# Another order for the head of a four-stage kernel: weights ahead of x, another order of the loads, ten warm-up calls

## The reference, cut to what matters

```
attn = (w1^T @ w2^T) * sparse_mask                       # 512 x 512
x = x + gelu(layernorm(x) @ attn + b2)                   # stage 1
x = x + ffn(layernorm(x))                                # stage 2
x = x + attention(layernorm(x); Wqkv, bqkv, Wo, bo)      # stage 3, one head of 128
x = x + ffn(layernorm(x))                                # stage 4

ffn(z): dots = softmax(z @ centroids.T / 0.1); hits = dots > 0.01
        rows where any hit, columns whose cluster was hit anywhere:
        z @ weight.T + bias, else 0
```

## Time and profile before

| | before |
|---|---|
| median of 3 runs | 275.45 us |
| the profiled execution, its own time | 275.24 us |
| its span | 273.4 us |
| TensorE busy | 268.8 us (98%) |
| DVE, ACT, POOL busy | 192.2, 177.0, 163.8 us |
| HBM read, written | 13.76 MB, 4.19 MB |

### The profile page before, as it was taken

The page is one execution under the profiler, slowest core; times in us unless marked ns, Lnnn a source line. Parts: engine busy times, 40 slices in busy tenths (PEclk is TensorE's granted clock), DMA queues, the critical chain, the costliest instruction groups (busy, mean ns, idle before and its releaser), DMA issues.

```text
span 273.4 us, 4428 instructions
## 1 busy us (share of the span) xinstructions
PE 268.8 (98%) x1397; PEld 225.6 (82%) x1397; DVE 192.2 (70%) x406; ACT 177.0 (65%) x359; POOL 163.8 (60%) x196
## 2 busy tenths in 40 slices
...
DMA packets 10247, 18.25 MB, mean 67 GB/s; under 512 B 1200, under 2 KB 1968, under 8 KB 10224
## 3 DMA queue, kind: packets, MB, share of 16 engines
...
HBM read 13.76 MB, written 4.19 MB: 66 GB/s over the span
## 4 chain that ended last, share of the span: by engine, by line
PE 96%; DMA 1%; DVE 1%; POOL 1%; issue 0%; ACT 0%; DVEq 0%; POOLq 0%
PE m_bank L1018 76%; PE t_bank L1113 12%; PE m_bank L1197 6%; PE t_bank L1119 1%; DMA x_tok<-in_L_attn_a_x 1%; PE m_bank L1073 1%; ACT xn_odd L613 0%; PE t_bank L1138 0%; DVE st L817 0%; POOL rstd L471 0%; POOL ve L470 0%; DVE y_tok L988 0%; DVE x_tok L994 0%; PE m_bank L1144 0%; PE t_bank L1124 0%
## 5 line engine op out<-in xcount | busy, mean ns | idle before, releaser
L1018 PE MATMUL m_bank<-ffn_hi,even_hi 128*128 128x512 f32 x96 | 38.9, 406 | 0.0
L1018 PE MATMUL m_bank<-ffn_lo,even_hi 128*128 128x512 f32 x96 | 37.6, 392 | 0.0
L1018 PE MATMUL m_bank<-ffn_hi,even_lo 128*128 128x512 f32 x96 | 37.4, 390 | 0.0
L602 ACT ACTIVATE ones_and_squares<-x_tok,mv 128x512 bf16<-128x512 f32 x44 | 31.6, 717 | 4.1 <-DVE x_tok L921 3.7
L559 POOL TENSOR_TENSOR y_tok<-y_tok,x_tok 128x512 f32<-128x512 f32 x12 | 15.3, 1289 | 25.6 <-ACT y_tok L755 25.6
L539 POOL TENSOR_TENSOR y_tok<-y_tok,bias_f 128x512 f32<-128x512 f32 x16 | 20.6, 1295 | 16.2 <-ACT y_tok L696 16.2
L467 POOL TENSOR_SCALAR ve<-mv 128x1 f32<-128x1 f32 (+1 forms) x20 | 5.3, 264 | 37.9 <-ACT ones_and_squares L602 36.9
L824 DVE TENSOR_TENSOR even_lo<-t_bank,even_hi 128x512 fp32r<-128x512 f32 x24 | 16.2, 684 | 12.8 <-ACT even_hi L645 12.6
L471 POOL TENSOR_TENSOR rstd<-ve,half 128x1 f32<-128x1 f32 (+1 forms) x31 | 23.5, 758 | 2.6
L824 DVE TENSOR_TENSOR odd_lo<-t_bank,odd_hi 128x512 fp32r<-128x512 f32 x28 | 18.8, 686 | 6.4 <-ACT odd_hi L645 6.2
L1018 PE MATMUL m_bank<-odd_hi,wqkv_hi 128*128 128x512 f32 (+1 forms) x60 | 21.5, 358 | 0.0
...
## 6 DMA issues: line engine op xcount, KB each, us to landing
...
```

The costliest lines, as they stand in the source:

```text
L602: act.activation(squares, x_tok[:, n, :], ACT.Square, bias=sum_of(*key), scale=-float(D), accum_out=mv[:, i, 1:2]).then_inc(done[kind], 1)
L1018: ins = pe.matmul(bank, a, w, start=(first and n == 0), stop=(last and n == count - 1))
```

## The change

`WARM` goes from 12 to 10 and five orders are rewritten in their first part. Every step keeps its code; the set of steps is the same. From `dn2.0.1.c21` on TensorE's, from `sq.2.1.2` on ACT's, from `onehot` on DVE's and from `rstd.2.0 ... xlo.2.0` on POOL's order are unchanged. The code of ACT's first load is rewritten without changing what it issues, but it is `load.w1.1` now. `BY_POOL` is the same set.

```diff
-WARM = 12
+WARM = 10
 PE_ORDER
-attn.0.0 T.x1.0.0 attn.0.1 attn.0.2 T.x1.0.1 attn.1 T.x1.0.2 last.0 last.1 last.2 last.3 T.x1.0.3 y1.0.0.c0
-y1.0.2.c0 y1.0.0.c2 T.cen.0.0 y1.0.2.c2 y1.0.3.c02 y1.0.0.c1 colmean y1.0.0.c3 y1.0.1.c3 ffnmean y1.0.2.c1
-y1.0.1.c2 y1.0.2.c3 y1.0.1.c10 y1.0.3.c31 y1.1.0.c02 T.x2.0.2 y1.1.0.c3 y1.1.2.c0213 y1.1.0.c1 T.x2.0.0
-y1.1.1.c231 y1.1.3.c132 y1.1.1.c0 T.x2.0.3 T.x2.0.1 dn2.0.2.c01 y1.1.3.c0 dn2.0.0.c10 T.x2.1.0 dn2.0.0.c2
-dn2.0.2.c23 dn2.0.3.c32 dn2.0.0.c3 dn2.0.3.c0 dn2.0.1.c21 dn2.0.3.c1 cl2.0.h01 T.x2.1.3 y1.2.0.c20 T.x2.1.1
+attn.0.0 attn.0.1 attn.0.2 attn.1 last.0 last.1 T.x1.0.2 last.2 last.3 T.x1.0.0 T.x1.0.1 T.x1.0.3 y1.0.2.c02
+y1.0.0.c201 y1.0.3.c0 colmean y1.0.0.c3 y1.0.1.c12 y1.0.2.c31 y1.0.3.c3 y1.0.1.c30 y1.0.3.c2 T.x2.0.0 T.x2.0.2
+y1.0.3.c1 y1.1.0.c01 ffnmean y1.1.1.c012 y1.1.0.c2 y1.1.3.c01 y1.1.0.c3 y1.1.3.c23 T.x2.0.1 y1.1.1.c3
+y1.1.2.c032 T.x2.0.3 y1.1.2.c1 dn2.0.0.c203 T.cen.0.0 dn2.0.2.c01 dn2.0.0.c1 T.x2.1.0 dn2.0.2.c23 dn2.0.3.c320
+dn2.0.1.c21 dn2.0.3.c1 cl2.0.h01 T.x2.1.3 y1.2.0.c20 T.x2.1.1 dn2.0.1.c30 T.x2.1.2 y1.2.0.c3 y1.2.3.c3 y1.2.0.c1
 ACT_ORDER
-w1hi.0 w2hi.0 norm.1.0.0 w1hi.1 norm.1.0.1 w2hi.1 w2hi.2 w1hi.2 w1hi.3 w2hi.3 norm.1.0.2 hi.x1.0.0 hi.x1.0.2
-hi.x1.0.1 rawhi.0 norm.1.0.3 rawhi.2 hi.x1.0.3 ccen rawhi.1 fshi rawhi.3 shi xhi.1.0 ahi.0 gelu.0.0 ahi.2 ahi.3
-gelu.0.2 ahi.1 hi.cen.0.0 xhi.1.2 sq.2.0.2 gelu.0.3 xhi.1.3 xhi.1.1 hi.x2.0.2 gelu.0.1 fhi.2 fhi.1 sq.2.0.0
-hi.x2.0.0 fhi.0 sq.2.0.3 gelu.1.0 sq.2.0.1 gelu.1.2 fhi.3 hi.x2.0.3 gelu.1.1 hi.x2.0.1 sq.2.1.2 gelu.1.3 xhi.2.0
+w1hi.0 w1hi.1 w2hi.0 w1hi.2 w2hi.3 w2hi.1 w2hi.2 w1hi.3 norm.1.0.3 norm.1.0.2 rawhi.0 hi.x1.0.2 norm.1.0.1
+norm.1.0.0 rawhi.2 rawhi.1 hi.x1.0.0 hi.x1.0.1 hi.x1.0.3 rawhi.3 shi ahi.0 ahi.1 gelu.0.0 xhi.1.0 gelu.0.2 fshi
+ahi.2 xhi.1.1 xhi.1.2 gelu.0.3 xhi.1.3 gelu.0.1 hi.x2.0.2 hi.x2.0.0 ahi.3 fhi.0 fhi.1 fhi.2 ccen sq.2.0.1
+gelu.1.0 fhi.3 gelu.1.1 hi.x2.0.1 sq.2.0.0 hi.x2.0.3 sq.2.0.3 gelu.1.3 hi.cen.0.0 sq.2.0.2 gelu.1.2 sq.2.1.2
 DVE_ORDER
-stats.1.0.0 w1lo.0 stats.1.0.1 stats.1.0.2 w2lo.0 stats.1.0.3 w1lo.1 w2lo.1 w2lo.2 w1lo.2 w1lo.3 w2lo.3
-lo.x1.0.0 cstat lo.x1.0.1 mask_attn.0 mask_attn.1 lo.x1.0.2 mask_attn.2 rawlo.0 rawlo.2 mask_attn.3 lo.x1.0.3
...
+w1lo.0 w1lo.1 w2lo.0 w1lo.2 w2lo.3 w2lo.1 stats.1.0.3 w2lo.2 w1lo.3 stats.1.0.2 stats.1.0.1 stats.1.0.0
+mask_attn.0 mask_attn.1 rawlo.0 lo.x1.0.2 mask_attn.2 cstat mask_attn.3 rawlo.2 lo.x1.0.0 lo.x1.0.3 rawlo.1
+rawlo.3 slo lo.x1.0.1 stats.1.1.3 center.0 center.1 scaled.0.0 center.2 stats.1.1.2 scaled.0.2 x1.0.0 x1.0.2
+scaled.0.1 fslo scaled.0.3 center.3 stats.1.1.1 stats.1.2.1 x1.0.3 stats.1.1.0 x1.0.1 fcent.1 fcent.0 fcent.2
+scaled.1.0 lo.x2.0.2 fcent.3 scaled.1.1 lo.x2.0.0 scaled.1.3 x1.1.0 x1.1.1 lo.x2.0.1 scaled.1.2 stats.1.2.3
+lo.cen.0.0 stats.1.3.3 x1.1.2 lo.x2.0.3 stats.1.2.0 x1.1.3 onehot stats.1.2.2 lo.x2.1.1 scaled.2.0 lo.x2.1.0
 POOL_ORDER
-rstd.1.0.0 rstd.1.0.1 rstd.1.0.2 rstd.1.0.3 fsum.1 fsum.2 fsum.3 asum.1 cmean asum.2 asum.3 alo.0 xlo.1.0 alo.2
-alo.3 xlo.1.2 alo.1 xlo.1.3 xlo.1.1 rstd.1.1 flo.0 latehi.2 flo.1 flo.2 rstd.2.0 flo.3 xlo.2.0 latehi.0 xlo.2.2
+rstd.1.0.3 rstd.1.0.2 rstd.1.0.1 rstd.1.0.0 asum.1 asum.2 asum.3 fsum.1 fsum.2 fsum.3 alo.0 alo.1 xlo.1.0
+xlo.1.1 alo.2 cmean xlo.1.3 alo.3 rstd.1.1 xlo.1.2 flo.1 flo.2 flo.0 flo.3 latehi.4 latehi.2 rstd.2.0 xlo.2.0
 SP_ORDER
-load.x0.0 load.w2.0 load.x0.1 load.x0.2 load.w1.1 load.x0.3 load.w2.1 load.w2.2 load.w1.2 load.w1.3 load.w2.3
-load.ffn.1 load.ffn.0 load.cen load.ffn.2 load.sparse.0 load.ffn.3 load.sparse.1 load.sparse.2 load.sparse.3
-load.small load.x.1 load.b2 load.xt.1 load.x.3 load.late load.x.2 load.bias load.xt.2 load.xt.3 store.0.1
+load.w1.0 load.w2.0 load.w1.2 load.w2.3 load.w2.1 load.w2.2 load.x0.3 load.w1.3 load.x0.2 load.x0.1 load.x0.0
+load.sparse.0 load.sparse.1 load.sparse.2 load.sparse.3 load.ffn.2 load.ffn.1 load.cen load.ffn.0 load.ffn.3
+load.x.1 load.b2 load.xt.1 load.x.3 load.bias load.x.2 load.small load.late load.xt.2 load.xt.3 store.0.1
-AQ_ORDER = "load.w1.0"
+AQ_ORDER: load.w1.1
```

More of the change, by code:

```diff
@@ L25 @@
 M_BANKS = 4
-WARM = 12
-BY_POOL = {(1, 3), (2, 3), (3, 2), (2, 2)}
+WARM = 10
+BY_POOL = {(1, 3), (2, 2), (2, 3), (3, 2)}
 SQUARED = {2, 3, 4}
 PE_ORDER = """
-attn.0.0 T.x1.0.0 attn.0.1 attn.0.2 T.x1.0.1 attn.1 T.x1.0.2 last.0 last.1 last.2 last.3 T.x1.0.3 y1.0.0.c0
-y1.0.2.c0 y1.0.0.c2 T.cen.0.0 y1.0.2.c2 y1.0.3.c02 y1.0.0.c1 colmean y1.0.0.c3 y1.0.1.c3 ffnmean y1.0.2.c1
-y1.0.1.c2 y1.0.2.c3 y1.0.1.c10 y1.0.3.c31 y1.1.0.c02 T.x2.0.2 y1.1.0.c3 y1.1.2.c0213 y1.1.0.c1 T.x2.0.0
-y1.1.1.c231 y1.1.3.c132 y1.1.1.c0 T.x2.0.3 T.x2.0.1 dn2.0.2.c01 y1.1.3.c0 dn2.0.0.c10 T.x2.1.0 dn2.0.0.c2
@@ new lines @@
+dn2.0.1.c21 dn2.0.3.c1 cl2.0.h01 T.x2.1.3 y1.2.0.c20 T.x2.1.1 dn2.0.1.c30 T.x2.1.2 y1.2.0.c3 y1.2.3.c3 y1.2.0.c1
+y1.2.3.c2 y1.2.2.c13 dn2.1.0.c1 y1.2.3.c10 y1.2.1.c3 y1.2.2.c0 y1.2.1.c1 y1.2.2.c2 dn2.1.0.c0 tc.2.0 dn2.1.2.c0
+y1.2.1.c02 dn2.1.0.c23 dn2.1.2.c312 cl2.1.h01 y1.3.3.c1 dn2.1.1.c02 y1.3.3.c3 dn2.1.3.c30 tc.2.1 y1.3.2.c1
+y1.3.3.c20 y1.3.2.c3 dn2.1.1.c3 y1.3.2.c2 dn2.1.3.c1 T.x2.2.0 dn2.1.1.c1 dn2.1.3.c2 T.x2.2.2 y1.3.2.c0 y1.3.1.c2
+T.x2.2.3 y1.3.1.c13 T.x2.2.1 y1.3.0.c1 y1.3.1.c0 y1.3.0.c302 T.x2.3.3 cl2.2.h01 T.x2.3.2 T.x2.3.1 dn2.2.3.c0
@@ new lines @@
+dn2.3.3.c3 dn2.2.3.c3 T.x2.3.0 tc.2.2 dn2.3.3.c1 dn2.2.3.c21 dn2.2.0.c2 cl2.3.h0 cl2.3.h1 dn2.2.2.c3 tc.2.3
+dn2.2.2.c1 dn2.2.0.c1 dn2.2.2.c2 dn2.2.0.c03 dn2.3.3.c20 dn2.2.2.c0 bestT.2 dn2.3.1.c2 mask.2 dn2.2.1.c1
+dn2.3.2.c3 dn2.3.1.c03 dn2.2.1.c2 dn2.3.2.c20 dn2.3.1.c1 dn2.3.2.c1 dn2.2.1.c0 T.x3.0.3 dn2.3.0.c13 T.x3.0.0
+dn2.3.0.c0 T.x3.0.2 dn2.3.0.c2 T.x3.0.1 dn2.2.1.c3 k.0.h1 k.0.h0 q.0.h0 q.0.h1 v.0.h1 T.x3.1.3 v.0.h0 sc.0.0
+T.x3.1.2 T.x3.1.1 sc.0.2 T.x3.1.0 T.v.0.0 sc.0.1 sc.0.3 T.p.0.0 q.1.h01 T.p.0.1 k.1.h01 T.p.0.2 T.p.0.3 v.1.h01
@@ new lines @@
+sc.1.3 T.x3.2.3 T.x3.2.0 sc.1.2 pv.0.h01 sc.1.0 sc.1.1 T.x3.2.1 T.v.1.0 T.x3.2.2 wo.0.0 wo.0.3 wo.0.2 T.p.1.0
+wo.0.1 T.p.1.1 k.2.h01 T.p.1.3 T.x4.0.0 T.p.1.2 q.2.h01 T.x4.0.3 T.x4.0.2 v.2.h01 pv.1.h01 sc.2.1 T.v.2.0
+T.x4.0.1 sc.2.2 wo.1.0 wo.1.2 T.x3.3.0 cl4.0.h01 wo.1.1 wo.1.3 tc.4.0 T.x3.3.2 sc.2.0 T.x3.3.3 T.p.2.1 sc.2.3
+dn4.0.1.c0 T.p.2.2 T.x3.3.1 dn4.0.3.c02 dn4.0.1.c2 T.p.2.3 dn4.0.3.c3 q.3.h01 dn4.0.1.c3 dn4.0.3.c1 T.p.2.0
+dn4.0.1.c1 k.3.h01 dn4.0.0.c0312 T.x4.1.0 sc.3.0 T.x4.1.1 dn4.0.2.c21 sc.3.2 dn4.0.2.c30 T.x4.1.3 sc.3.3
@@ new lines @@
+T.x4.1.2 pv.2.h01 sc.3.1 v.3.h01 T.p.3.2 T.p.3.3 wo.2.3 cl4.1.h01 wo.2.2 dn4.1.3.c0 tc.4.1 wo.2.0 dn4.1.0.c32
+T.p.3.0 dn4.1.3.c1 dn4.1.0.c0 T.v.3.0 T.p.3.1 dn4.1.2.c3 dn4.1.3.c32 dn4.1.2.c102 dn4.1.0.c1 T.x4.2.2 T.x4.2.3
+T.x4.2.0 wo.2.1 pv.3.h01 dn4.1.1.c012 wo.3.2 wo.3.0 dn4.1.1.c3 T.x4.2.1 wo.3.3 T.x4.3.0 T.x4.3.2 wo.3.1
+cl4.2.h01 T.x4.3.1 T.x4.3.3 tc.4.2 dn4.2.3.c2 cl4.3.h0 dn4.2.1.c1 cl4.3.h1 dn4.2.1.c2 tc.4.3 dn4.2.1.c3
+dn4.2.3.c1 dn4.2.1.c0 dn4.3.0.c2 dn4.2.3.c0 dn4.3.0.c0 dn4.2.3.c3 dn4.3.0.c31 bestT.4 dn4.3.2.c2 tmask.4 masks.4
@@ L62 @@
+dn4.3.2.c031 dn4.2.2.c0123 dn4.3.1.c0123 dn4.2.0.c0123 dn4h.3.3.0 dn4h.3.3.1
 """
 ACT_ORDER = """
-w1hi.0 w2hi.0 norm.1.0.0 w1hi.1 norm.1.0.1 w2hi.1 w2hi.2 w1hi.2 w1hi.3 w2hi.3 norm.1.0.2 hi.x1.0.0 hi.x1.0.2
-hi.x1.0.1 rawhi.0 norm.1.0.3 rawhi.2 hi.x1.0.3 ccen rawhi.1 fshi rawhi.3 shi xhi.1.0 ahi.0 gelu.0.0 ahi.2 ahi.3
-gelu.0.2 ahi.1 hi.cen.0.0 xhi.1.2 sq.2.0.2 gelu.0.3 xhi.1.3 xhi.1.1 hi.x2.0.2 gelu.0.1 fhi.2 fhi.1 sq.2.0.0
-hi.x2.0.0 fhi.0 sq.2.0.3 gelu.1.0 sq.2.0.1 gelu.1.2 fhi.3 hi.x2.0.3 gelu.1.1 hi.x2.0.1 sq.2.1.2 gelu.1.3 xhi.2.0
@@ new lines @@
+norm.1.0.0 rawhi.2 rawhi.1 hi.x1.0.0 hi.x1.0.1 hi.x1.0.3 rawhi.3 shi ahi.0 ahi.1 gelu.0.0 xhi.1.0 gelu.0.2 fshi
+ahi.2 xhi.1.1 xhi.1.2 gelu.0.3 xhi.1.3 gelu.0.1 hi.x2.0.2 hi.x2.0.0 ahi.3 fhi.0 fhi.1 fhi.2 ccen sq.2.0.1
+gelu.1.0 fhi.3 gelu.1.1 hi.x2.0.1 sq.2.0.0 hi.x2.0.3 sq.2.0.3 gelu.1.3 hi.cen.0.0 sq.2.0.2 gelu.1.2 sq.2.1.2
+xhi.2.0 ev2.0.2 xhi.2.2 sq.2.1.0 ev2.0.0 lgev.2.0 xhi.2.3 hi.x2.1.3 ev2.0.3 ev2.0.1 hi.x2.1.1 hi.x2.1.0 sq.2.1.1
+xhi.2.1 gelu.2.0 hi.x2.1.2 xhi.3.0 gelu.2.3 xhi.3.3 gelu.2.2 xhi.3.2 sq.2.1.3 ev2.1.0 gelu.2.1 sq.2.2.0 lgev.2.1
@@ L73 @@
+ev2.1.2 cexp.2.0 sq.2.2.1 xhi.3.1 sq.2.2.3 gelu.3.3 sq.2.2.2 hi.x2.2.0 hi.x2.2.2 ev2.1.1 sq.2.3.3 gelu.3.2
+ev2.1.3 hi.x2.2.3 hi.x2.2.1 sq.2.3.2 gelu.3.1 hi.x2.3.3 gelu.3.0 cexp.2.1 lgev.2.2 hi.x2.3.1 sq.2.3.0 hi.x2.3.2
 hi.x2.3.0 sq.2.3.1 ev2.2.3 cexp.2.2 lgev.2.3 cexp.2.3 ev2.3.3 ev2.2.0 ev2.2.2 norm.3.0.3 rows ev2.3.1 norm.3.0.0
```

75 lines of the change are left out of this document (29 added, 46 removed).

## The result

The changed kernel took 278.24 us, the median of four runs (277.91 to 279.61), against 275.47 for the kernel before beside it (275.39 to 275.65): ratio 1.0111, 95% interval 1.0081 to 1.0141. The forecast was 275.1 and its range ended at 276.9, so the time is 1.3 us outside it. The profiled execution took 278.45 us with a span of 276.4, 3.0 more than before.

The account below looks back on a forecast made before the run. TensorE, 96% of the chain that ended last, bounds the kernel; only its start and gaps can move. −0.77 (start) + 0.40 (T.cen loop) = −0.37 on the 275.45 median gives 275.1 us; range with rivals 274.6 to 276.9.

Parts of the forecast that it names:

- Part 1: Head of the kernel: TensorE's first products start earlier and a hole goes, a gain of 0.77 us.
- part 3: Near 50 us: TensorE waits for DVE's x1.1.3 to free a PSUM bank, 0.40 us lost (0 to 0.9).
- the walk of the orders: After the head: summed step times showed slo, fsum, x.2 and others in time; put at 0, allowing 0 to 0.6.
- part 2: Loads, ACT, DVE and POOL keep up with the earlier start; put at 0, with 0 to 0.6 for thin margins.
- The rule on VectorE and GpSimd: Skill page, applied at POOL's rstd chains: two-SBUF-input VectorE instructions shut out GpSimd reading SBUF; by it that stall is 0.
- The start: First product at 5.80, attn.1 through at 11.60 instead of 12.37: 0.77 us gained, or 0.65 with w2hi.0 ending at 5.92.
- The 0.68 us grid of landings: Early weight loads: a 262 KB chunk takes 0.68 us at 0.39 MB per us, giving each load's landing time.
- The loop of T.cen: Near 50 us: T.cen to x1.1.3 takes 4.79 us against TensorE's own 4.39, a wait of 0.40 us.
- Rival (b): Before the first product: a TensorE hole delays the clock's rise; 277.5 us, or 276.3 for half; chance 0.13.
- Rival (c): POOL at 9.3 to 13 us: slow rstd chains make T.x1.0.2 up to 2.1 late; 277.2 or 275.6; chance 0.11.
- (d): DVE's stats.1.2.1 near 33 us: x.2 lands late, at 35.1, x1.0.3's bank late by 1.0; 276.1 us; chance 0.06.
- (e): Small waits at the 0.3 us margins of the walked orders beyond what was allowed: 275.9 to 276.3 us; chance 0.10.

Follow-up runs that it names:

- Experiments 1 to 3: Changed kernel with fsum waiting for slo: 275.27 us; fsum on one column: 275.23; fsum as two memsets: 275.25; fsum as two copies: 275.81.
- both edits: Changed kernel with POOL's first fsum waiting for slo and DVE's x1.1.3 ahead of lo.cen.0.0, no TensorE wait left: 274.70 us, ratio 0.9966 against the kernel before.
- experiment 7: Later fsum and earlier x1.1.3 in the changed kernel, plus twelve warm-up calls: 274.80 us; plus four: 275.86; plus w2.1 as SP's third load: 274.73.

## Why the prediction was wrong

Part 1 and part 3 of the prediction held in their mechanism; the walk of the orders in part 2 did not. The step that failed is in part 2, "Further on I walked the orders with these steps (0.61 a DVE operation ...)", with its result that slo is done at 22.2 for a colmean at 23.0 and that fsum "now stands behind asum on POOL, until 24.3", priced at 0. I had moved fsum to where DVE subtracts SBUF from SBUF three times and looked only for who waits for fsum, not for whom fsum shuts out. Experiments 1 to 3 show this place: in place of 0.61, the three DVE operations came 1.7 us apart (20.71, 22.45, 24.14), 3 × 1.1 us in all; slo was done at 25.9 for the forecast 22.2, and 2.6 us (with restarts 2.8) reached TensorE. Without the contention the walk was right: in the trace of both edits slo is done at 22.4. The rule on VectorE and GpSimd stood in the same part, one paragraph up, and was applied to POOL's small operations alone, as the one that loses. The traces show that whichever has started first makes the other wait. In the kernel before that was DVE, and POOL's asum.2 took 1.77 us for 1.3:

```profile
19.45 0.69 DVE L803 TENSOR_TENSOR wqkv_lo<-y_tok,wqkv_hi 128x512 fp32r<-128x512 f32 x1
...
19.53 3.20 POOL L489 TENSOR_TENSOR y_tok<-y_tok 128x512 f32<-128x512 f32 x2
```

In the changed kernel, at rawlo.1, it was POOL, by 0.03 us, and after that the two alternated.

The other steps:

- *The start, −0.77.* Right in its mechanism. attn.1 was to be through at 11.60; it was at 11.73 in the version without waits, whose chain is 0.63 ahead, and at 11.92 in the changed kernel's trace, where 0.45 remained. There TensorE was ready for attn.1 at 8.49, earlier than the 8.85 forecast, as the slow first products were missing; w2lo.1 was done at 8.97 for 8.48, so the 0.37 us of cover became a wait of 0.53. SP's third load (w1.2) landed near 6.3 in place of 5.6, and what followed on ACT with it. The 0.68 us grid of landings was the mis-sized term here.
- *Ten calls for twelve.* With the other edits in, the first product came at 5.60 with ten calls and at 5.90 with twelve; in the time that gave nothing (experiment 7).
- *The loop of T.cen, +0.40.* Right in place and mechanism: 0.46 in the trace and 0.1 for the restart. T.cen stood at 48.76 and x1.1.3 on DVE 4.13 us behind it, for 4.07 forecast:

```profile
52.89 0.66 DVE L864 SCALAR_TENSOR_TENSOR x_tok<-m_bank,x_tok 128x512 f32<-128x512 f32 x1
```

- *Rival (b), the clock.* It did not come in, but this trace doesn't test it: the clock had risen before the hole. Its 20 warm-up passes took 4.14 us (the row at 0.97), against 4.63 with both edits, whose piece of the chain and first products are:

```profile
0.97 4.63 PE m_bank L1006 x20
...
5.60 1.74 PE L1070 MATMUL m_bank<-w2t_hi,even_hi 128*128 128x512 f32 x4
```

  In the changed kernel the passes start 0.21 us apart until 4.5 us and 0.11 apart from there; then comes the hole of 0.5, then four products in 1.17. With both edits all passes are 0.21 apart, there are 0.2 us of idleness at most, and yet the products stay slow until about 6.9. So the place of the rise moved by 2.4 us between traces with the same ten calls and nearly the same unbroken work ahead of it. Four calls with 2.6 us of idleness put it at 8.8, later than in any other trace; which of the two did it, the fewer calls or the hole, no run separates. The prediction took one trace's 6.46 as fixed.
- *Rival (c), slow rstd chains.* The first was slow, 1.8 us (10.04 to 11.86), as forecast, the last too, 1.7 (14.61 to 16.33), and TensorE did not wait; the two between took 1.3.
- *Rivals (d), (e).* x.2 was there in time; the margins of 0.3 us after 27 us all held.

The upper side of the range was set by these rivals, and none was a stretched DVE, so 278.2 had no case at all.
